# A recurrence of 128 steps on one core: the engines' loops hold 24 steps instead of three, with eight in front instead of five

## What is computed

```python
def step(S, inp):
    qt, kt, vt, bt, gt = inp
    S = S * jnp.exp(gt)[..., None, None]
    for i in range(nh):                      # nh = 3
        ki, vi, bi = (kt[:, :, i], vt[:, :, i], bt[:, :, i])
        kS = jnp.einsum('bhd,bhde->bhe', ki, S)
        S = S + bi[..., None, None] * (ki[..., None] * (vi - kS)[:, :, None, :])
    o = jnp.einsum('bhd,bhde->bhe', qt, S)
    return (S, o)
xs = tuple((jnp.moveaxis(a, 1, 0) for a in (q, k, v, beta, g)))
_, o = jax.lax.scan(step, S0, xs)
```

## Time and profile before

| | |
|---|---|
| median of 3 runs | 5299.64 us |
| lowest and highest | 5281.81, 5305.36 us |
| the profiled execution's own time | 5270.66 us |
| span in its profile (first to last instruction) | 5268.9 us |
| mean granted TensorE clock (1 is 2.4 GHz) | 0.949 |
| first and last body's end on VectorE (line 1093) | 157.5 and 4251.3 us |
| PE busy | 4693.9 us (89%) |
| DVE busy | 3705.6 us (70%) |
| ACT busy | 3669.7 us (70%) |
| POOL busy | 1049.0 us (20%) |

### The profile page before, as it was taken

The page is one execution under the profiler, slowest core; times in us unless marked ns, Lnnn a source line. Parts: engine busy times, 40 slices in busy tenths (PEclk is TensorE's granted clock), DMA queues, the critical chain, the costliest instruction groups (busy, mean ns, idle before and its releaser), DMA issues. The chain is left out here.

```text
span 5268.9 us, 152499 instructions
## 1 busy us (share of the span) xinstructions
PE 4693.9 (89%) x50692; PEld 4103.3 (78%) x50692; DVE 3705.6 (70%) x9813; ACT 3669.7 (70%) x9026; POOL 1049.0 (20%) x975
## 2 busy tenths in 40 slices
PE   1899999999999999999999999999999976599993
PEld 0788888888888888888888888888888865488882
DVE  3787778778788788787787787787877742244446
ACT  2787877778787787778787777787777741155552
POOL 2112222222222222222222222221111101300004
PEclk6999999999999999999999999999999989799996
DMA  4222222222222222222222222222222213266664
GB/s 197 75 57 69 69 70 72 75 64 79 68 73 69 69 69 69 69 69 69 69 71 80 63 80 65 73 60 55 55 55 55 55 42 109 90 235 230 229 236 144
DMA packets 322339, 474.76 MB, mean 90 GB/s; under 512 B 85888, under 2 KB 267136, under 8 KB 302720
## 3 DMA queue, kind: packets, MB, share of 16 engines
q1 hardware_dynamic: 304784, 436.99, 28.5%
q0 software_dynamic: 6144, 16.79, 1.0%
q10 hardware_dynamic: 10608, 10.23, 0.6%
HBM read 351.96 MB, written 107.75 MB: 87 GB/s over the span
## 5 line engine op out<-in xcount | busy, mean ns | idle before, releaser
L1085 DVE SCALAR_TENSOR_TENSOR conv_acc<-bank,c_cur,conv_acc 128x256 f32<-128x256 f32 x2688 | 1283.0, 477 | 27.2 <-ACT conv_acc L898 4.6
L607 PE MATMUL bank<-x_cur,w_cur 128*128 128x259 f16 (+1 forms) x6144 | 855.2, 275 | 71.5 <-DMA g_cur<-g_parts 66.9
L955 ACT ACTIVATE inv<-bank 128x256 f16<-128x256 f32 x1536 | 608.2, 396 | 262.7 <-PE bank L702 241.2
L607 PEld LDWEIGHTS bank<-x_cur,w_cur 128*128 128x128 f16 (+1 forms) x6144 | 588.9, 102 | 138.8 <-DMA g_cur<-g_parts 67.8
L1141 DVE CAST_PREDICATED xs_lev<-mask,bank 128x256 f16<-128x256 uint16 x1536 | 657.5, 428 | 46.0 <-PE bank L691 4.2
L753 PE MATMUL bank<-state,kq_t 128*128 128x128 f32 x2048 | 482.7, 318 | 118.7 <-issue 84.9
L1246 POOL TENSOR_TENSOR squares<-kq_t 128x1024 f32<-128x1024 f32 x128 | 242.7, 1896 | 1689.9 <-ACT kq_t L910 1689.9
L1148 DVE SCALAR_TENSOR_TENSOR rhs<-bank,t_cur,v_rows 128x128 f32<-128x128 f32 x1024 | 352.3, 344 | 264.4 <-issue 151.2
L963 ACT ACTIVATE invt<-bank 128x256 f16<-128x256 f32 x1280 | 508.9, 398 | 23.0
L898 ACT ACTIVATE conv_acc<-bank,c_cur 128x256 f32<-128x256 f32 x896 | 423.6, 473 | 127.2 <-PE bank L607 126.9
L1154 DVE SCALAR_TENSOR_TENSOR state<-state,t_cur,bank 128x128 f32<-128x128 f32 x1024 | 351.9, 344 | 214.3 <-PE bank L775 210.7
(11 more groups left out here) (247 smaller groups left out, 11300.2 us busy)
## 6 DMA issues: line engine op xcount, KB each, us to landing
w_cur<-w_parts_scratch SPq DMA_DIRECT2D x128, 1024.0 KB, 6.8
ew<-e_parts_scratch SPq DMA_DIRECT2D x117, 896.0 KB, 6.1
x_cur<-x_parts_scratch SPq DMA_DIRECT2D x128, 259.0 KB, 7.1
x_slots<-no_rows SPq DMA_DIRECT2D x128, 256.0 KB, 6.4
e_parts_scratch<-e_pair SPq DMA_DIRECT2D x96, 224.0 KB, 2.8
y_scratch<-y_buf SPq DMA_DIRECT2D x128, 128.0 KB, 1.8
y_in<-y_scratch SPq DMA_DIRECT2D x32, 512.0 KB, 3.9
rows<-x_slots SPq DMA_DIRECT2D x39, 256.0 KB, 5.5
```

The source lines that it names most:

```text
L607: last = mm(bank[c % 2][:, 0:PW], w_cur[res][:, wp, k, c * P:(c + 1) * P].bitcast(BF16 if wp else F16), x_cur[res][:, xp, k, 0:PW].bitcast ...
L955: a(half(inv[g][:], l, 0), packed(halves(bank[4 + g]), l), ACT.Copy).then_inc(t_kept, 1)
L1085: v.scalar_tensor_tensor(acc, bank[c % 2][:, i:i + TB], c_cur[res][:, c, i:i + 1], acc, ALU.mult, ALU.add).then_inc(tap_step if i < TAPS - ...
```

## The change

`run_bodies` calls the same bodies with the same order inside. Eight of them stand in front of the loop, and the loop holds 24: (128 - 8) / 24 = 5 rounds, with 4 edges. The loop's line becomes 463. The loops of SyncE and GpSimd, all tiles, semaphores and work are as before.

```diff
-PEELED = 5
+PEELED = 8
+UNROLL = 24
...
                 for n in range(peeled):
                     body(n, n // RING, n % RING)
-                rounds = (NIT - peeled) // RING
-                assert peeled + rounds * RING == NIT
+                rounds = (NIT - peeled) // UNROLL
+                assert peeled + rounds * UNROLL == NIT and UNROLL % RING == 0
                 with eng.Fori(0, rounds) as m:
-                    for i in range(peeled, peeled + RING):
-                        turn = m + i // RING
-                        body(RING * turn + i % RING, turn, i % RING)
+                    for i in range(peeled, peeled + UNROLL):
+                        body(UNROLL * m + i, UNROLL // RING * m + i // RING, i % RING)
                 for n in range(NIT, NIT + STAGES - 1):
                     body(n, n // RING, n % RING)
```

## The result

| | before | with the change |
|---|---|---|
| median | 5302.5 us (4 runs) | 5145.78 us (4 runs) |
| lowest and highest | 5281.81, 5308.53 us | 5139.37, 5148.14 us |
| ratio | | 0.9709, 95% interval 0.9681 to 0.9737 |
| the profiled execution's own time | 5270.66 us | 5148.14 us |
| between the first and the last end of a body (L1093) | 4093.8 us | 3932.0 us |

The kernel is 2.9% faster. The forecast was 5111 us in a range of 5075 to 5150.

What follows compares the result with a forecast made beforehand. TensorE bounds each 30.7 us body, and jumps back (edges) add 4.98 us each. Removing 36 saves 179.3 us, ScalarE adds 4: -175.3, giving 5124.3 or 5098 us, middle 5111, range 5075 to 5150.

Steps and rivals of the forecast that it cites:

- Edges taken away: Jumps back of the body loop: 40 become 4, and 36 at 4.98 us each go, 179.3 us saved.
- Edges that stay: Four jumps back, at bodies 32, 56, 80 and 104, each left at 4.98 us for TensorE and VectorE.
- The bound above: Upper limit for a remaining jump back: 8.1 us, from the seventh edge, 12.5 us more over the four.
- ScalarE's edges: ScalarE may wait at its four jumps: 1 us each, 4 in all; nothing if its branch takes TensorE's median 4.3 us.
- Straight code at nothing: Three engines stream new instructions through every body; costed at nothing, since the first five straight bodies take 30.8 us each.
- SyncE's and GpSimd's edges: Their jumps every 12 bodies, partly at bodies 44, 68, 92 without a TensorE jump: nothing, with over 20 us to spare.
- The sum: Whole kernel: -179.3 + 4 = -175.3 us, the fall expected between the first and last L1093.
- The 29 us between the profiled execution and the median: Whole kernel: outside the edges the new median is 5124.3 us, inside them 5098; the middle, 5111, was taken.
- the forecast's own range: Whole kernel: 5080 to 5145 us for the main case, which had a chance of 0.90.
- Every third body: Rival: the loss belongs to each turn of the buffer rings, not the jump; 5300 us, chance 0.03.
- Late straight code: Rival: every second of 120 bodies loses 1.82 us on TensorE to a late page; 5220 us, chance 0.05.
- The clock: Rival: without pauses TensorE is held at 1.2 GHz; from 6 of 120 bodies on the gain is gone; chance 0.01.

Runs made afterwards that it cites:

- full_unroll: The changed kernel with all 128 bodies as straight code on TensorE, ScalarE and VectorE, no loop: 5097.0 us, 0.9621 of the kernel before.
- peel8_loop3: The changed kernel with its loop cut from 24 bodies to 3, still behind eight: 5349.1 us, 1.0105 of the kernel before.
- tensor_pad64: The changed kernel with 64 idle semaphore increments on TensorE's queue ahead of the loop: 5114.5 us, 0.9680 of the kernel before.
- early_loads_before: The kernel before, with SyncE's loads of the next body issued ahead of its wait for the state: 5406.2 us, 1.0236 of the kernel before.
- before_again: The kernel before, unchanged, measured and profiled once more: 5293.7 us, ratio 1.0001.
- the second occasion: The changed kernel, unchanged, measured again beside the kernel before: 5117.0 us against 5290.2 us, ratio 0.9677.
- early_loads_after: The changed kernel, with SyncE's loads of the next body issued ahead of its wait for the state: 5162.1 us, 0.9768 of the kernel before.
- scalar_keeps_3: The changed kernel with ScalarE alone keeping its old loop of 3 bodies behind five: 5138.3 us, 0.9692 of the kernel before.

## Why the prediction was right, and where it was off

**What bounds the kernel.** Right. A body costs 30.7 us whether it is straight or in the loop, and the edges were the only loss: full_unroll ends at 3894.8 us, 199.0 us below before, where the prediction had 199.0 from the branches' starts.

**Edges taken away, -179.3 us.** Right in mechanism and number of edges. The Trainium skill, "Advanced Engine Details and Errata", section Control Flow Timing, gives about 108 ns for a compare-and-branch. By that all 40 edges would be worth 4 us; full_unroll took 199 us away, and the measurement decides. Only the branches' own rows on ScalarE and VectorE and TensorE's last, which falls through, are that short, 40 to 83 ns.

**Edges that stay, at 4.98 us each.** This is the step that was off. They cost 8.3 us: 33.4 in place of 20 us. The bound above, 8.1 us an edge, was passed by two of the four (11.6 and 10.1 us), and three had a wait for "issue" some ten microseconds into the body, which the prediction had named as a sign of being wrong. I had taken an edge's price as a property of the engines and of what SyncE loads meanwhile. It also depends on where the loop's head lies in the instructions, and the change moved the head by three bodies. peel8_loop3 and tensor_pad64 show it from both sides.

**ScalarE's edges, +4 us.** The direction was right and shown (2.8 us behind its branch in place of 0.2); the price is about nothing. The prediction's reasoning for the median case, that it is back before TensorE needs it, is what happened. Its reason for the wait, the length of the loop, is not: peel8_loop3 has the wait with a loop of three, so the three bodies in front are enough for it. Whether a loop of 24 behind five bodies would wait, no run shows.

**Straight code at nothing.** Right for this order of transfers: in full_unroll TensorE's matmuls have no wait for "issue" in the stretch, and VectorE's add up to 1.3 us. The rows shown for it were those of q14 alone. The same view has TensorE's q8 with 16 packets in the 160 us of straight code and 9 in the 86 us inside the loop, about one in 10 us in both: TensorE was streaming its instructions in the old loop already, a better reason for the nothing. early_loads_before shows that it is not free whatever SyncE does. Without the edges' excess the stretch is 3898.6 us in the changed kernel (3932.0 - 33.4) and 3894.8 us in full_unroll; I don't know where these 4 us come from.

**SyncE's and GpSimd's edges.** Right: no spacing stands out at bodies 44, 68 and 92.

**The sum.** The stretch fell by 161.8 us, the prediction said 175.3. The difference is 13.5 us: 9.5 from the edges (33.4 against 23.9 with ScalarE's share) and the other 4 from the spacings away from them.

**The 29 us between the profiled execution and the median.** The prediction took the middle between "in the edges" and "outside". They were mostly outside: before_again has the same edges within 6 us, and its span is 22 us longer in all, of which 13.5 lie behind the last body, 6 in the stretch and 2 ahead of it. So 5124 us was the better base, and 5111 was too low by a choice that the trace gave no ground for. With the stretch's 13.5 us this gives 5138, 8 us short of 5145.8; the part behind the last body moves by more than this between executions, so I don't look for a cause. The errors had the same sign: 5145.8 lies just above the 5145 of the forecast's own range and 4 us inside the whole one. The lower end of that own range doesn't follow either, as 5098 less 5.5 and 18 is 5074.5 and not 5080. On the second occasion the medians were 173 us apart, in place of 157, nearer to the 175.3 of the sum.

**The rivals.** Every third body: excluded. Late straight code: not here, but real in the early_loads kernels. The clock: the granted clock was 1.00 from 1165 to 1850 us, from 1910 to 2595 and from 2655 to 3340, the straight parts of three rounds. The rival on the slower side that I did not name is the one that exists: with the same 8 bodies in front and a loop of three, the kernel is 1.05% slower than before.

## What to carry to other kernels

When a trace shows straight bodies all alike and "issue" at a jump back, multiply what a body with a jump takes longer by the jumps: here 40 times 5.0 us. It is more than the idle time (84.9 us at L753), because the clock falls behind a stop. Full unrolling won all of it here, since the straight code was fetched in time. Count the edges that stay at a price of their own, since moving a loop's head took an edge here from 5.0 to 7.0 us (three bodies) and from 8.3 to 3.2 us (64 instructions). Look at which transfers start within ten microseconds of a jump, and before moving them, at which fetch they would then delay.

## What the runs showed of the hardware that I had not expected

Instruction packets are late while data is loading. In the change no packet of TensorE's instruction queue came in 10 us while x_cur and w_cur were loading and data took 60.6% of the DMA engines' time, and TensorE stood still for 4.8 us. With the loads moved away (early_loads_after) the second packet behind a jump came after 4.3 to 4.6 us instead of 7.3 to 12.6.

Behind a jump one packet of 16 KB comes to TensorE after 1.0 to 1.6 us, and the next one 7.3 us or more behind the branch in the change. Whether the first lasts until then depends on where the loop's head lies: 64 instructions of shift took an edge from 8.3 to 3.2 us.

ScalarE passed a jump back in 0.24 us with a loop of three bodies behind five (scalar_keeps_3), and in 2.5 to 3.1 us with the same loop behind eight (peel8_loop3). VectorE, with a loop of three too, waited 2.8 to 9.4 us before. The Trainium skill, "Runtime: NRT & Kernel Launch", section Instruction fetch mechanics, says that a target outside what is held on chip has to be fetched; the waits agree, and ScalarE's pair shows that the length of a loop alone doesn't tell whether its target is held. No run here finds the size or the place at which it begins.
